# Last convolution of a four-layer kernel: the f16 high part written once by ScalarE, its second copy made by GpSimd

## The chip, the cores and the metric

The kernel runs on one core of a Trainium2 chip. The metric is the device time of the program in microseconds. The core has TensorE (PE, with its weight loads as PEld), VectorE (DVE), ScalarE (ACT), GpSimd (POOL) and SyncE (SP); the last here only issues transfers.

## The reference, cut to what matters

Four residual layers act on x of 8 x 16 x 512 x 512 (images, channels, rows, columns). The stage that is changed computes the third and the fourth:

```
# --- layer 2: quantized 3x3 convolution of the normalized x ---
x = x + _L2_conv_ref(_gn(x), weight_int8, scale_weight, bias)
# --- layer 3: multiplication in the frequency domain, by a 3x3 kernel, circularly padded ---
w_pad = _circular_pad(weight, H, W, k, p)
Lw = jnp.fft.fft2(w_pad * dL)
Kx = jnp.fft.ifft2(x, norm='ortho')
z = jnp.einsum('oihw,bihw->bohw', Lw, Kx)
x = x + jnp.real(jnp.fft.fft2(z, norm='ortho'))      # x inside is _gn(x)
```

The fourth layer is thus a 3x3 convolution with circular borders over the normalized x. The kernel computes it as one.

## The kernel before, in words

The first two thirds of the time (to about 4487 us) are the first two layers and statistics; the change doesn't touch them. The last stage handles the third layer (called conv2 in the code) and the fourth (conv3) for all eight images. An image is J = 64 tiles of 128 partitions (8 rows of 16 channels) by 512 columns, and X in SBUF holds one image.

A hand-written order of turns staggers the work. In turn t of image b, ScalarE, VectorE, TensorE and SyncE each do what belongs to several tiles: conv3 of image b runs over t, and conv2 of image b + 1 runs DELAY = 12 turns behind. So the first 12 turns of an image have conv3 alone, the last 12 conv2 alone, and image 7 has conv3 alone throughout. Between two images the statistics of the next are finished (var, rstd, norm3_ready). There is nothing but these functions and their semaphores; each engine runs its own in order.

Turn t on each engine, for conv3:

- ScalarE: `high` (L1551) writes the f16 high part of xn, item t - 1, into planes 0 and 2 of ring buffer `xs3` (8 slots); `normal` (L1543) writes xn of item t (f32, two buffers), after `low` of item t - 2. For conv2: `scale2` (L1529) before `high`, `load` (L1558, in every other turn, two tiles of the next image, into the X that conv3 has finished with) and `square3` (L1535) after `normal`.
- GpSimd: `circular` (L1509, L1510) copies the two border columns of xn, each as a product with a column of ones. `high` waits for it (pads3_ready).
- VectorE: `finish` (L1669, result tile, waits for conv3 and for the stored result buffer), `update` (L1656, conv2's result), `clip` (L1646), `low` (L1662: xn minus the high part, plane 1 of xs3), `quant` (L1651).
- SyncE: in odd turns `halos3`: waits for low and high of item t - 1, then transfers rows of neighbouring tiles from xs3, all three planes, into `xhalo` (L1462, L1470; L1459 at an image's first tile, L1464 to L1468 with the wrapped tile); in even turns `halos2` for conv2 (L1447, L1448); in every turn then `store` (L1476) of a finished result tile.
- TensorE: `conv2` (L1600, L1601: 4 matmuls) and `conv3` (L1613: 9 matmuls of xs3, with its planes 0 and 1; L1615: 3 of xhalo) of tile t - 6. It takes a halo half from three turns before.

So plane 2 is read by the halo transfers alone. `high` may be at most 7 tiles ahead of conv3 (conv3_done), xn has two buffers, the result four, conv3's PSUM two banks.

## Time and profile before

| | before |
|---|---|
| median of three runs | 6585.06 us (6578.19 to 6588.43) |
| profiled execution | 6585.46 us, of which the span is 6583.6 |
| busy, share of the span | PE 87%, DVE 75%, ACT 69%, POOL 41% |
| the changed line, L1551 | 520 times, 1049 ns in the mean |
| high part of the first image, last image | from 4596.9 us, to 6560.5 us |

The profile page gives the busy time of each engine, of the span in 40 slices, the transfer queues, a chain of waits followed back from the end, and groups of instructions by line. The span counts from the first to the last instruction. A matmul's recorded duration is longer than its share of the pipeline, so durations of matmuls are added only over a stretch. The chain of the page follows GpSimd through this stage as "issue" and L1509, since the inference goes by semaphores; it says little here, and the timeline is the better view.

### The profile page before, as it was taken

The numbers are of one execution on the slowest core, as the hardware profiler recorded it, in microseconds if no ns is written. First come the engines' busy times: TensorE is split into PE (matmuls) and PEld (weight loads), VectorE is DVE, ScalarE is ACT, GpSimd is POOL, SyncE is SP. The second block draws the span as 40 slices with busy tenths as digits, with TensorE's granted clock in tenths as the row PEclk, the third lists the DMA queues.
The fourth block names the chain that finished last, engine by engine and source line by source line (L and its number), as shares of the span: only waits on it lengthen the run. The fifth ranks groups of instructions, "written<-read, shape, count | busy, mean of one in ns | idle before, by whom it ended". The sixth has DMA issues, their size and how long they took to land. (4 is left out here: it accounts for less than half of the span.)

```text
span 6583.6 us, 201217 instructions
## 1 busy us (share of the span) xinstructions
PE 5696.3 (87%) x64138; PEld 3661.9 (56%) x64138; DVE 4922.5 (75%) x9721; ACT 4531.8 (69%) x8793; POOL 2724.0 (41%) x4633
## 2 busy tenths in 40 slices
PE   0389979979979989989988988994989889889889
PEld 0058748748848757756766766771433334334334
DVE  5778877877887887887887887887767667667664
ACT  2577767767767766766766547556878778778776
POOL 2165556556556555556546546550111111111111
PEclk9899989989999999999999999997999999999999
DMA  6426616615625634643642541552767667667665
GB/s 182 169 59 185 186 41 187 185 54 177 185 75 157 185 99 133 184 124 105 185 145 67 142 130 48 143 141 43 196 168 198 167 167 203 163 170 202 169 172 137
DMA packets 535623, 959.19 MB, mean 146 GB/s; under 512 B 121946, under 2 KB 126682, under 8 KB 532826
## 3 DMA queue, kind: packets, MB, share of 16 engines
q1 hardware_dynamic: 467546, 799.21, 43.9%
q10 hardware_dynamic: 67456, 151.01, 7.1%
q8 instruction: 474, 7.77, 0.5%
q14 instruction: 147, 1.20, 0.1%
HBM read 560.66 MB, written 287.60 MB: 129 GB/s over the span
## 5 line engine op out<-in xcount | busy, mean ns | idle before, releaser
L1613 PE MATMUL pC<-xs,taps 128*128 128x512 f16 x4608 | 1094.3, 382 | 105.9 <-DMA xhalo<-xs 101.4
L966 PE MATMUL pM<-gw,xh 64*128 64x256 f16 (+1 forms) x24960 | 1128.7, 244 | 0.0
L966 PEld LDWEIGHTS pM<-gw,xh 64*128 64x128 f16 x24960 | 966.8, 95 | 129.7 <-issue 3.3
L728 POOL TENSOR_TENSOR X<-X,zo 128x256 f32 (+1 forms) x512 | 371.5, 726 | 1244.1 <-DVE X L1077 1244.1
L1613 PEld LDWEIGHTS pC<-xs,taps 128*128 128x128 f16 x4608 | 448.8, 98 | 668.8 <-DVE xs L1662 88.3
L1509 POOL TENSOR_TENSOR xn<-xn,one_col 128x1 f32<-128x1 f32 x520 | 159.4, 307 | 1401.0 <-ACT xn L1543 1401.0
L1529 ACT ACTIVATE scaled<-X,qbias,qscale 128x512 f32 (+1 forms) x512 | 411.0, 804 | 344.9 <-DMA X<-after_layer 284.7
L272 PE MATMUL pM<-X,mix0s 64*64 64x512 f32 x2304 | 528.4, 633 | 133.9 <-DVE X L1049 108.3
L1077 DVE SCALAR_TENSOR_TENSOR X<-pZ,X 128x512 f32 (+1 forms) x512 | 353.8, 691 | 327.3 <-ACT zo L787 326.1
L1551 ACT ACTIVATE xs<-xn 128x1028 f16<-128x1028 f32 x520 | 545.7, 1049 | 73.5 <-POOL xn L1510 72.2
L713 POOL TENSOR_TENSOR X<-X,rl 128x512 f32 x384 | 478.2, 1275 | 269.4 <-ACT rl L758 269.0
L787 ACT ACTIVATE zo<-pZ 128x256 f32<-128x256 f32 x512 | 196.7, 384 | 551.1 <-PE pZ L918 551.1
L1669 DVE SCALAR_TENSOR_TENSOR result<-pC,X 128x512 f32<-128x512 f32 x512 | 352.1, 688 | 297.5 <-DMA out_dram<-result 205.7
L1600 PE MATMUL pC<-q,taps 128*128 128x512 f16 x1536 | 436.5, 394 | 126.4 <-DMA qhalo<-q 98.5
L1091 DVE TENSOR_TENSOR xt<-pT,xt 128x512 f16<-128x512 f32 x520 | 357.0, 686 | 250.5 <-ACT xt L817 248.5
L1662 DVE TENSOR_TENSOR xs<-xn,xs 128x514 f16<-128x514 f32 x520 | 359.5, 691 | 228.1 <-ACT xs L1551 224.1
L817 ACT ACTIVATE xt<-pT 128x512 f16<-128x512 f32 x520 | 310.6, 597 | 283.8 <-PE pT L930 280.2
L272 PE MATMUL pP<-X,sumw 64*64 64x512 f32 x2048 | 465.7, 593 | 0.0
L758 ACT ACTIVATE rl<-pM,relu_b,relu_s 128x512 f32<-128x512 f32 x384 | 285.4, 776 | 248.1 <-DVE X L1043 234.7
L918 PE MATMUL pM<-fwd_odd,xt 128*128 128x256 f16 x3120 | 436.2, 277 | 5.6 <-DVE xh L1102 5.6
L1543 ACT ACTIVATE xn<-X,bs,rs 128x512 f32 (+1 forms) x520 | 416.7, 801 | 32.7 <-DVEq L1708 24.2
L838 ACT ACTIVATE yt<-pM 128x512 f16<-128x512 f32 x520 | 311.1, 598 | 174.1 <-PE pM L974 173.2
(241 smaller groups left out, 13755.0 us busy)
## 6 DMA issues: line engine op xcount, KB each, us to landing
gw<-row_weights SPq DMA_DIRECT2D x520, 288.0 KB, 3.1
after_layer<-X SPq DMA_DIRECT2D x512, 256.0 KB
out_dram<-result SPq DMA_DIRECT2D x512, 256.0 KB
X<-in_x_dram SPq DMA_DIRECT2D x448, 256.0 KB
X<-after_layer ACTq DMA_DIRECT2D x224, 512.0 KB, 5.8
stage<-in_x_dram SPq DMA_DIRECT2D x192, 512.0 KB
xhalo<-xs SPq DMA_DIRECT2D x504, 96.4 KB, 3.7
qhalo<-q SPq DMA_DIRECT2D x496, 96.2 KB, 4.0
```

The costliest lines, as they stand in the source:

```text
L272: return nc.tensor.matmul(dst[c * HP:(c + 1) * HP], left, Xf[r * HP:(r + 1) * HP, j], start=start, stop=stop)
L713: nc.gpsimd.tensor_tensor(Xf[:, j], Xf[:, j], rl[:, k], ALU.add).then_inc(added_pool, 1)
L728: nc.gpsimd.tensor_tensor(X[:, j, 0], X[:, j, 0], zo[:, k], ALU.add)
L918: m = nc.tensor.matmul(dst, left(p), right(q), start=first and n == 0, stop=last and n == 2)
L966: nc.tensor.matmul(pY[:, r, col:col + nd * P], row(xh, r)[:, k, p, ri, off:off + P], weights(r, q_, d, nd, ri), start=ri == 0 and off == 1 ...
L1091: nc.vector.tensor_tensor(xt[:, k, 1], pT[:, :], xt[:, k, 0], ALU.subtract).then_inc(xt_lo, 1)
L1529: nc.scalar.activation(scaled[:, k % 4], Xf[:, w], ACT.Identity, bias=qbias[:, bass.ds(b, 1)], scale=qscale[:, bass.ds(b, 1)]).then_inc(sc ...
L1543: nc.scalar.activation(xn[:, k % 2, 1:W + 1], Xf[:, tile], ACT.Identity, bias=bs3[:, :], scale=rs3[:, :]).then_inc(xn_ready, 1)
L1551: nc.scalar.activation(xs[:, 0:3:2, k], xn[:, (k - 1) % 2].unsqueeze(1).broadcast_to([P, 2, W + 2]), ACT.Copy).then_inc(hi_ready, 1)
L1600: nc.tensor.matmul(pC2[:, slot % 4], taps2[:, d], q[:, k, d:d + W], start=d == 0, stop=False)
L1613: nc.tensor.matmul(bank, taps3[:, d, wh], xs[:, h, own, d:d + W], start=d == 0 and n == 0, stop=False)
L1662: nc.vector.tensor_tensor(xs[:, 1, k], xn[:, (k - 1) % 2], xs[:, 0, k], ALU.subtract).then_inc(lo_ready, 1)
```

## The change

`high` writes plane 0 alone (514 elements a partition instead of 1028). A new function `again` on GpSimd waits for it and writes plane 2 as plane 0 times a column of ones, broadcast over 514 columns; it stands ahead of `circular` of the next item. `halos3` waits for `again` where it waited for `high`. The wait for `low` stays. The whole diff:

```
@@ -1398,6 +1398,7 @@
                     s_("xn3_ready"), s_("pads3_ready"), s_("hi3_ready"), s_("lo3_ready"), s_("conv3_done"), s_("x4_ready"))
                 xhalo_in = [s_(f"xhalo_in{k}") for k in range(4)]
                 wrap_in = s_("wrap_in")
+                again_ready = s_("again3_ready")
                 out_stored = [s_(f"out_stored{k}") for k in range(4)]
                 loaded2 = [s_(f"loaded2_{k}") for k in range(2)]
                 CONV2_CREDIT = RING - 1
@@ -1454,7 +1455,7 @@
 
                         src = (k - 1) % RING
                         sp.wait_ge(lo_ready, b * ITEMS + t)
-                        sp.wait_ge(hi_ready, b * ITEMS + t)
+                        sp.wait_ge(again_ready, b * ITEMS + t)
                         if isinstance(t, int) and t == 1:
                             sp.dma_start(xhalo[0:3 * C, 1], xs[P - C:P, :, 1]).then_inc(xhalo_in[0], 16)
                             return
@@ -1510,13 +1511,20 @@
                         nc.gpsimd.tensor_tensor(xn[:, k, W + 1:W + 2], xn[:, k, 1:2], one_col[:, :],
                                                 ALU.mult).then_inc(pads3_ready, 1)
 
+                    def again(b, i, slot):
+                        pool.wait_ge(hi_ready, b * ITEMS + i + 1)
+                        nc.gpsimd.tensor_tensor(xs[:, 2, slot], xs[:, 0, slot], one_col[:, :].broadcast_to([P, W + 2]),
+                                                ALU.mult).then_inc(again_ready, 1)
+
                     with pool.Fori(0, B) as b:
                         pool.wait_ge(var_ready, b + 1)
                         nc.gpsimd.tensor_tensor(rstd[:, :], var[:, 1:2], half_pow[:, :], ALU.pow).then_inc(rstd_done, 1)
                         circular(b, 0, 0)
                         with pool.Fori(0, J // RING) as g:
                             for k in range(RING):
+                                again(b, g * RING + k, (k + 1) % RING)
                                 circular(b, g * RING + k + 1, (k + 1) % 2)
+                        again(b, J, 1)
 
                 @block.scalar
                 def _(act):
@@ -1548,7 +1556,7 @@
                         if not (isinstance(i, int) and i < RING):
 
                             act.wait_ge(conv3_done, b * J + i - (RING - 1))
-                        nc.scalar.activation(xs[:, 0:3:2, k], xn[:, (k - 1) % 2].unsqueeze(1).broadcast_to([P, 2, W + 2]), ACT.Copy).then_inc(hi_ready, 1)
+                        nc.scalar.activation(xs[:, 0, k], xn[:, (k - 1) % 2], ACT.Copy).then_inc(hi_ready, 1)
 
                     def load(b, w, k, g):
 
```

## Rows read from the trace of the kernel before

**Rows 1.** Windows of an image and the last: us, busy and count by engine, PEclk, DMA.
```profile
5928.00:5966.00 38.00, 35.15 (x160) 15.30 (x160) 27.00 (x59) 29.22 (x45) 4.81 (x20) 1.00 0.76 197
5966.00:6110.00 144.00, 142.40 (x655) 63.19 (x656) 109.21 (x247) 126.52 (x206) 22.39 (x78) 1.00 0.75 207
6445.00:6575.00 130.00, 130.00 (x602) 58.26 (x601) 62.17 (x96) 85.02 (x91) 14.92 (x90) 1.00 0.59 141
```

**Rows 2.** Waits of ScalarE (total, times, longest); timeline (start, us) of loads and scaled.
```profile
ACT scaled L1529 <- DMA X<-after_layer: 284.7, 167, 5.3
...
5913.97 0.81 ACT L1529 ACTIVATE scaled<-X,qbias,qscale 128x512 f32<-128x512 f32 x1 [0.78 <-DMA X<-after_layer]
5914.55 0.40 ACTq L1558 DMA_DIRECT2D X<-after_layer  x1
...
5920.58 0.81 ACT L1529 ACTIVATE scaled<-X,qbias,qscale 128x512 f32<-128x512 f32 x1 [1.61 <-DMA X<-after_layer]
```

**Rows 3.** Timeline of an image's start, conv3 alone.
```profile
5893.52 1.06 ACT L1551 ACTIVATE xs<-xn 128x1028 f16<-128x1028 f32 x1 [0.44 <-POOL xn L1510]
...
5895.36 0.19 POOL L1509 TENSOR_TENSOR xn<-xn,one_col 128x1 f32<-128x1 f32 x1 [1.88 <-ACT xn L1543]
...
5895.73 1.06 ACT L1551 ACTIVATE xs<-xn 128x1028 f16<-128x1028 f32 x1 [0.44 <-POOL xn L1510]
...
5898.27 3.94 PE L1613 MATMUL pC<-xs,taps 128*128 128x512 f16 x9 [12.64 <-DMA xhalo<-xs]
```

**Rows 4.** Groups by line and form (busy us, mean ns); L336: min/median/max ns.
```profile
L1551 ACT ACTIVATE xs<-xn 128x1028 f16<-128x1028 f32 x520 | 545.7, 1049 | 73.5 <-POOL xn L1510 72.2 <-PE pC L1615 0.5
...
L787 ACT ACTIVATE zo<-pZ 128x256 f32<-128x256 f32 x512 | 196.7, 384 | 551.1 <-PE pZ L918 551.1
...
L1543 ACT ACTIVATE xn<-X,bs,rs 128x512 f32<-128x512 f32 x200 | 160.1, 800 | 24.7 <-DVEq L1708 24.2 <-DVE xs L1662 0.5
...
L336 POOL TENSOR_TENSOR gbuf<-comph,maskh x64: 1145/1147/1323, 11.7 to 223.3; 128x576 f16<-128x576 f16 x64
...
L713 POOL TENSOR_TENSOR X<-X,rl 128x512 f32 x384 | 478.2, 1275 | 269.4 <-ACT rl L758 269.0
```

**Rows 5.** GpSimd beside VectorE: timeline at 439 us, one group, timeline at 4655 us.
```profile
439.11 0.69 DVE L1067 TENSOR_TENSOR zo<-zo,rhi 128x512 f32<-128x512 f32 x1
439.49 0.90 POOL L717 TENSOR_TENSOR even<-rl 128x256 f32<-128x256 f32 x1 [3.26 <-ACT rl L773]
439.83 0.83 DVE L1068 TENSOR_SCALAR zo<-zo,lo_slot 128x512 f32<-128x512 f32 x1
...
L728 POOL TENSOR_TENSOR X<-X,zo 128x256 f32 x448 | 325.0, 726 | 1051.7 <-DVE X L1077 1051.7
...
4655.32 0.69 DVE L1662 TENSOR_TENSOR xs<-xn,xs 128x514 f16<-128x514 f32 x1
4655.41 0.65 POOL L1510 TENSOR_TENSOR xn<-xn,one_col 128x1 f32<-128x1 f32 x1
```

**Rows 6.** Timeline of the last image.
```profile
6401.00 1.06 ACT L1551 ACTIVATE xs<-xn 128x1028 f16<-128x1028 f32 x1 [0.44 <-POOL xn L1510]
...
6560.48 1.06 ACT L1551 ACTIVATE xs<-xn 128x1028 f16<-128x1028 f32 x1 [0.44 <-POOL xn L1510]
...
6564.21 0.64 SPq L1462 DMA_DIRECT2D xhalo<-xs  x1
...
6570.48 2.11 PE L1613 MATMUL pC<-xs,taps 128*128 128x512 f16 x9
```

**Rows 7.** Transfers, 4600 to 6390 us: count, KB, median us to landing.
```profile
xhalo<-xs SPq DMA_DIRECT2D x441, 96.4 KB, 3.8
```

**Rows 8.** VectorE, a turn in the middle of an image: clip, finish, clip.
```profile
5980.26 0.42 DVE L1646 TENSOR_SCALAR scaled<-scaled 128x512 f32<-128x512 f32 x1
...
5981.87 0.69 DVE L1669 SCALAR_TENSOR_TENSOR result<-pC,X 128x512 f32<-128x512 f32 x1 [0.25 <-DMA out_dram<-result]
...
5983.14 0.42 DVE L1646 TENSOR_SCALAR scaled<-scaled 128x512 f32<-128x512 f32 x1
```

More of the change, by code:

```diff
@@ L1400, in program @@
                 wrap_in = s_("wrap_in")
+                again_ready = s_("again3_ready")
                 out_stored = [s_(f"out_stored{k}") for k in range(4)]
@@ L1456, in halos3 @@
                         sp.wait_ge(lo_ready, b * ITEMS + t)
-                        sp.wait_ge(hi_ready, b * ITEMS + t)
+                        sp.wait_ge(again_ready, b * ITEMS + t)
                         if isinstance(t, int) and t == 1:
@@ L1511, in circular, with again @@
                                                 ALU.mult).then_inc(pads3_ready, 1)
+                    def again(b, i, slot):
+                        pool.wait_ge(hi_ready, b * ITEMS + i + 1)
+                        nc.gpsimd.tensor_tensor(xs[:, 2, slot], xs[:, 0, slot], one_col[:, :].broadcast_to([P, W + 2]),
+                                                ALU.mult).then_inc(again_ready, 1)
                     with pool.Fori(0, B) as b:
@@ L1518, in _ @@
                             for k in range(RING):
+                                again(b, g * RING + k, (k + 1) % RING)
                                 circular(b, g * RING + k + 1, (k + 1) % 2)
+                        again(b, J, 1)
                 @block.scalar
@@ L1550, in high @@
                             act.wait_ge(conv3_done, b * J + i - (RING - 1))
-                        nc.scalar.activation(xs[:, 0:3:2, k], xn[:, (k - 1) % 2].unsqueeze(1).broadcast_to([P, 2, W + 2]), ACT.Copy).then_inc(hi_ready, 1)
+                        nc.scalar.activation(xs[:, 0, k], xn[:, (k - 1) % 2], ACT.Copy).then_inc(hi_ready, 1)
                     def load(b, w, k, g):
```

## The prediction

> **What bounds the kernel now.** I read the busy shares by slice first: only the last quarter (from 4490 us) has the change in it, and there TensorE is busy, GpSimd idle. Then the windows of one image, which show the same thing in numbers: in the middle of the image TensorE is busy for 142.4 of 144 us, ScalarE 126.5, VectorE 109.2, GpSimd 22.4 [rows 1]. A turn (one tile of the last convolution and one of the next image's third layer) is 16 matmuls, so it costs 142.4 / 655 x 16 = 3.48 us of TensorE; that is the floor of the middle, and it is nearly reached. The earlier stretch has 2.85 us of idle TensorE in 38 [rows 1]. The two windows hold 182 us with 4.45 of idle TensorE; over the some 220 us between an image's first matmul and its tail, that makes 5.4.
>
> What else is tight was read from the waits of ScalarE: its longest is for the load of X, 284.7 us over the seven images that load [rows 2]. The timeline shows the ring: scaled at 5913.97, the next load issued at 5914.55, the next scaled released by that load at 5920.58 after 1.61 us of idling, and so on [rows 2]. Scaled, the high part (L1551), xn (L1543) and the squares follow one another on ScalarE; where it waits for a load, a shorter L1551 buys nothing.
>
> At the start of an image there is no third-layer work for 12 turns. The timeline shows another ring there: high part at 5893.52, then xn on ScalarE, the two border columns on GpSimd from 5895.36, the next high part at 5895.73 [rows 3]: 2.21 us a turn, and TensorE's first matmuls come at 5898.27, after 12.64 us of idling for the halo [rows 3]. In the last image too there is no other layer: 12 matmuls a turn, 130.0 / 602 x 12 = 2.59 us [rows 1].
>
> **What is removed.** 520 times L1551 goes from 1028 to 514 elements. It costs 1.049 us; a Copy of 256 costs 0.384 [rows 4], so (1.049 - 0.384) / 772 = 0.86 ns an element and 0.61 us for 514. The other end is L1543, 512 elements in 0.80 us [rows 4]; I take 0.61, from the row of the same line. That is 0.44 us a turn off ScalarE, in total 229 us of busy time, nearly all beside other work: ScalarE has 126.5 / 144 of the middle and waits for loads.
>
> **What is added.** 520 products of 128x514 on GpSimd, f16 by a broadcast column of f32. No such instruction is in the trace. Below: the f16 product of 576 elements, 1.147 us, scaled to 1.02. Above: the f32 sum of 512, 1.275 [rows 4], 1.28. The new one has one operand of each kind; I take the middle, 1.15. A gain is excluded: the instruction is new, and GpSimd does nothing shorter for it.
>
> The Trainium skill (GPSIMD Engine Reference, Instruction dispatch) gives about 2.5 cycles an element at 1.2 GHz as the floor of two-input operations, by which 514 elements would be an estimated 1.07 us of loop alone and the whole about 1.28. The f16 row lies under that floor (1.147 for 576), so the trace disagrees for f16; by the page the sum below would end at its upper bound.
>
> **How it shares with VectorE.** The timeline around 439 us is the row that matters most: L717 on GpSimd is issued at 439.49 while VectorE's L1067, with two SBUF inputs, runs to 439.80, and ends at 440.39, 0.59 us after it; and L1068 on VectorE, issued at 439.83, ends 0.27 us after L717 has [rows 5]. They take turns whole, and the one that waits goes next. An instruction of its size alone takes 0.73 (L728), so 0.14 us of a GpSimd instruction is hidden while it queues. In the stage itself a one-column product issued at 4655.41, normally 0.19 us, took 0.65, up to just after the end of low (L1662, 4655.32 to 4656.01), and before quant [rows 5].
>
> The new copy and low are released by the same high part. So: high 0.61, gap 0.03 (as between 439.80 and 439.83 [rows 5]), low 0.69, copy 1.15 - 0.14 = 1.01, border columns and gap, 5895.36 to 5895.73, 0.37 [rows 3]: the ring is **2.71 us** instead of 2.21. It holds whichever of low and copy goes first. With 1.02 and 1.28 for the copy it is 2.58 and 2.84.
>
> **Start of each image.** From the first high part to turn 12 are 11 rings: 11 x 0.50 = 5.5 us. From this comes the 0.78 us that scaled then waited for its load anyway [rows 2]: the load ring starts 4.7 us later. TensorE needs less: it goes at 2.59 a turn, so it would have overtaken the old ring only by little, and its halos came in time. Ends: nothing, if TensorE's lead hides it all, and 4.7. I take 3.5, nearer to the upper end since the load ring, too, runs at about TensorE's pace and gives nothing back; seven images: **24.5 us**.
>
> **Last image.** First high part at 6401.00, the last (64 rings later) at 6560.48 [rows 6]. By the new ring: 6401.0 + 64 x 2.71 = 6574.4. Low and copy bring the halo transfer's issue to 6574.4 + 0.61 + 0.03 + 0.69 + 1.01 = 6576.8 (before: 6564.21), landing 3.8 later by the median [rows 7], 6580.6. Tile 62, which needs it, began at 6570.48 [rows 6]: **10 us** later. With 2.58: 2 us; with 2.84: 18.
>
> **The new wait.** SyncE waited for low and high; now for low and copy, 1.01 us later where low goes first. Queued behind it on SyncE are the two halo transfers (three at an image's end, with the wrap one) and then the store of a result tile. Halos are wanted three turns later, 10.4 us, against 3.8 landing, so the middle hides it. The store is tighter: L1669 already waited 0.25 us for an out_dram transfer at 5981.87 [rows 8]. But VectorE has slack in every turn (below). On GpSimd the border columns are queued behind the copy, and the next high part behind these; in the middle, again 2.71 plus one quant (about 0.3), 3.0 < 3.48: hidden, at 0 us. If TensorE's cover went, this ring would be the floor. On VectorE, quant stands behind the copy by about 1 us; qhalo follows from it, wanted three turns later as well.
>
> **Sum.** 24.5 + 10 = 34.5. The profiled execution took 6585.46 us (span 6583.6, 1.9 around it), the median is 6585.06; they stand 0.4 apart, so the sum is laid on the median: 6585 + 35 = **6620 us**, 0.5% slower. Its own range: with a copy of 1.02 (ring + 0.37) and half of the lag hidden, 7 x 0.5 x (11 x 0.37 - 0.78) + 2 = 13; with 1.28 (ring + 0.63) and none hidden, 7 x (11 x 0.63 - 0.78) + 18 = 61: 6598 to 6646.
>
> **Rivals.** *Absorbed:* TensorE's queue of finished tiles hides the slower ring at each start and nearly all of it in the last image; then only some us are left and the time is 6585, within 13. For it: TensorE is the bound [rows 1]; against: in the last image the new ring is over TensorE's turn by itself.
>
> *Faster:* ScalarE catches up sooner after each late load, so the 5.4 us of TensorE pauses in an image shrink to 1.4: 7 x 4 = 28 us less, and the start ring costs little since the copy turns out short: 6557. Against it: the pauses go with the load (L1529's wait), not with L1551.
>
> *Slower, through VectorE:* every copy holds back clip, low or quant for its whole 1.01 us. A turn of VectorE back to back is 5980.26 to 5983.14 less 0.25 of waiting, 2.63 [rows 8]; with the copy 3.64, over TensorE's 3.48. The point from which it decides is 0.85 us of holding a turn. Some 53 turns of seven images at 0.16: 59 us, and the 35 above: 6679. For it: the whole-instruction turns of [rows 5]; against it: finish and update, 5981.87 to 5983.14 [rows 8], 1.27 us of a turn, have one operand in PSUM by the code, unlike L1067 and L1068, and a late VectorE moves the copy into them. The Trainium skill (SBUF — State Buffer, Who interferes with whom) says the same of the pair: an exclusive lock, the second to issue fully blocks, also for a VectorE instruction with two SBUF inputs against a GpSimd one that reads. By that rule, the trace agrees, and by its letter alone this rival's time would hold.
>
> *Not what it says:* the broadcast operand makes the copy far dearer, 2 us say; then the ring is 3.6 us, over every floor, and the time beyond 6700.
>
> **How the numbers follow.** Forecast 0.45, absorbed 0.20, faster 0.13, through VectorE 0.18, dear copy 0.04. About 0.2% (13 us) is what a measurement of this kernel can tell from no change. Faster by more 0.13; within 0.19 (the absorbed case, little of the forecast's lower end); slower 0.68. The range leaves out the dear copy and half of the faster case and holds the rest: 6565 to 6690; it takes in the VectorE case with 11 us to spare.
>
> **What would show it.** Starts of high parts in the first ten turns 2.71 us apart instead of 2.21 (right), 2.2 (absorbed). The copy's mean between 1.02 and 1.28. GpSimd's copy beginning with or just after low and ending about 1.0 after low's end. In the last image pairs of high parts 5.4 apart and TensorE idle for the halo; in the middle TensorE still at 3.48 a turn. Low or quant well over their 0.69 and 0.42 while TensorE idles would show the VectorE case. The forecast is wrong if GpSimd reads a broadcast or mixed operands at another rate, or if the slower start costs TensorE more than the delay itself: its first nine matmuls after the pause took 3.94 us [rows 3], twice the 9/12 x 2.59 = 1.94 of later ones [rows 1], and more pauses could prolong that.

## The result, and the profile after

The changed kernel takes 6639.8 us against 6582.6 us of the kernel before in the same session: ratio 1.0083, 95% interval 1.0068 to 1.0098. It is 57 us slower by the medians and 55 by the ratio; 6620 was forecast, from 6565 to 6690. The profiled execution of after took 6637.14 us, with a span of 6634.9.

The page of the kernel after: span, busy time by engine, and the groups of the copy (L1516), the high part (L1559), low (L1670) and finish (L1677); behind the bar stand the busy time, the mean in ns, and the idle time before with what ended it.

```profile
span 6634.9 us, 201809 instructions
...
L1516 POOL TENSOR_TENSOR xs<-xs,one_col 128x514 f16<-128x514 f16 x520 | 649.6, 1249 | 728.9 <-ACT xs L1559 728.9
...
L1559 ACT ACTIVATE xs<-xn 128x514 f16<-128x514 f32 x520 | 325.1, 625 | 208.6 <-POOL xn L1511 198.9
...
L1670 DVE TENSOR_TENSOR xs<-xn,xs 128x514 f16<-128x514 f32 x520 | 398.5, 766 | 164.8 <-ACT xs L1559 138.1
...
L1677 DVE SCALAR_TENSOR_TENSOR result<-pC,X 128x512 f32<-128x512 f32 x512 | 350.6, 685 | 246.1 <-DMA out_dram<-result 231.9
```

The high part went from 1049 ns to 625 as forecast (0.61), and ScalarE now idles before it for the border columns of GpSimd 198.9 us, where it was 72.2 [rows 4]. The same windows of an image and of the last one as in [rows 1], 31 and 47 us later, since the image itself is later (us, then busy time and count of PE, PEld, DVE, ACT, POOL, then clock, DMA share, GB/s):

```profile
5959.00:5997.00 38.00, 36.02 (x166) 15.71 (x165) 33.77 (x57) 25.48 (x45) 21.29 (x33) 1.00 0.76 198
5997.00:6141.00 144.00, 135.99 (x622) 59.23 (x621) 124.02 (x235) 107.04 (x196) 75.92 (x118) 1.00 0.74 195
6492.00:6622.00 130.00, 130.00 (x600) 57.32 (x599) 75.46 (x98) 63.32 (x95) 86.67 (x142) 1.00 0.59 137
```

ScalarE has become 19 us lighter in the 144, GpSimd 54 heavier, and VectorE 15 us heavier though it has not one instruction more. TensorE is busy for 136.0 of 144 instead of 142.4: the middle of the image, which the forecast had left untouched, loses time. The last image stays full.

So that each stretch can be compared, I cut every kernel's trace at the same four events: the first high part of an image, the first matmul of the last convolution on tile 11 and that on tile 64, and the next image's first high part. "Start" is the first stretch summed over the seven images that have a neighbour, "middle" the second, "tail" the third, "last" runs from the last image's first high part to the end of its last `finish`. TensorE's floor of the middle is 53 turns x 7 x 3.48 = 1291 us. "Ring" is the distance of high parts in an image's first ten turns. All of it is one profiled execution each, the last two columns are from the timed runs.

| kernel | ring | start | middle | tail | last | median us | ratio, 95% |
|---|---|---|---|---|---|---|---|
| before | 2.23 | 281.9 | 1324 | 198 | 178.2 | 6582.6 | 1 |
| after | 2.61 | 307.8 | 1345 | 198 | 182.3 | 6639.8 | 1.0083 (1.0068 to 1.0098) |
| e1 border columns first | 2.1 | 282.5 | 1323 | 198 | 178.7 | 6585.3 | 1.0003 (0.9989 to 1.0017) |
| e2 copy aside | 2.61 | 306.7 | 1339 | 204 | 182.8 | 6641.7 | 1.0088 (1.0065 to 1.0112) |
| e3 copy of 2 | 1.9 | 262.5 | 1329 | 200 | 177.7 | 6569.0 | 0.9975 (0.9961 to 0.9989) |
| e11 no copy | 1.9 | 265.1 | 1337 | 199 | 177.5 | 6565.8 | 0.9976 (0.9966 to 0.9986) |
| e12 copy twice | 3.61 | 389.0 | 1458 | 204 | 249.3 | 6896.8 | 1.0482 (1.0462 to 1.0503) |
| e4 quant first | 2.61 | 303.0 | 1310 | 195 | 183.0 | 6581.3 | 0.9984 (0.9970 to 0.9998) |
| e5 before, quant first | 2.24 | 288.8 | 1308 | 198 | 178.0 | 6567.2 | 0.9971 (0.9957 to 0.9985) |
| e8 border and quant first | 2.1 | 284.4 | 1317 | 198 | 178.6 | 6574.6 | 0.9985 (0.9974 to 0.9995) |
| e6 split transfers | 1.9 | 269.6 | 1292 | 196 | 179.0 | 6538.7 | 0.9940 (0.9922 to 0.9958) |
| e7 split, quant first | 1.9 | 266.0 | 1319 | 200 | 177.1 | 6570.4 | 0.9980 (0.9971 to 0.9989) |
| e9 before, extra ahead of quant | 2.23 | 291.2 | 1395 | 211 | 178.4 | 6701.3 | 1.0177 (1.0162 to 1.0193) |
| e10 before, extra behind quant | 2.23 | 290.1 | 1354 | 208 | 178.2 | 6654.9 | 1.0105 (1.0088 to 1.0122) |

Each ratio is against the kernel before on the same chip, so two kernels of the table are best compared by their ratios; 0.001 is 6.6 us. From before to after the start takes 25.9 us more, the last image 4.1 and the middle 21; with the tails (0.4 less) and the stretch ahead of the first high part (0.7 more) that is the 51.3 us between the two profiled spans. A single execution is a rough gauge of the middle: the profiled one of e11 stands 15 us over its own median, that of e4 11. So I also use the timed runs: what is left of a median's difference once start and last image are taken off it. For after that is 57.2 - 25.9 - 4.1 = 27.2 us by the medians. The middle therefore costs 21 to 27, where 27 is a remainder and no measurement of its own.

**The start.** The timeline of after (start, us, engine, line; in brackets the idle time before and what ended it):

```profile
5919.61 0.63 ACT L1559 ACTIVATE xs<-xn 128x514 f16<-128x514 f32 x1 [0.44 <-POOL xn L1511]
...
5922.18 0.63 ACT L1559 ACTIVATE xs<-xn 128x514 f16<-128x514 f32 x1 [1.24 <-POOL xn L1511]
...
5924.76 0.63 ACT L1559 ACTIVATE xs<-xn 128x514 f16<-128x514 f32 x1 [1.24 <-POOL xn L1511]
...
5925.42 0.69 DVE L1670 TENSOR_TENSOR xs<-xn,xs 128x514 f16<-128x514 f32 x1 [1.88 <-ACT xs L1559]
5925.47 1.55 POOL L1516 TENSOR_TENSOR xs<-xs,one_col 128x514 f16<-128x514 f16 x1 [0.74 <-ACT xs L1559]
5926.98 0.18 POOL L1510 TENSOR_TENSOR xn<-xn,one_col 128x1 f32<-128x1 f32 x1
5927.12 0.18 POOL L1511 TENSOR_TENSOR xn<-xn,one_col 128x1 f32<-128x1 f32 x1
5927.34 0.63 ACT L1559 ACTIVATE xs<-xn 128x514 f16<-128x514 f32 x1 [1.24 <-POOL xn L1511]
...
5930.04 4.02 PE L1621 MATMUL pC<-xs,taps 128*128 128x512 f16 x9 [13.43 <-DMA xhalo<-xs]
```

In these turns it is the forecast's ring: high part, low and copy together, border columns, next high part, 2.58 us a turn instead of 2.21 [rows 3]. Low and the copy are released by the same event and begin within 0.05 us; the copy ends at 5927.02, 0.91 us after low. Then come L1510 and L1511, and 0.04 us after these the high part. TensorE's first matmuls come after 13.43 us of idling instead of 12.64. Of the rest, a good part reaches TensorE through VectorE: conv3 must wait until `finish` has emptied its bank, and `finish` is queued behind low. Within the seven starts TensorE's pauses for `finish` grow from 4.4 to 14.2 us, those for the two halos from 72.4 to 85.3.

**The last image.** Timeline of after:

```profile
6448.11 0.63 ACT L1559 ACTIVATE xs<-xn 128x514 f16<-128x514 f32 x1 [0.44 <-POOL xn L1511]
...
6478.00 2.11 PE L1621 MATMUL pC<-xs,taps 128*128 128x512 f16 x9 [1.28 <-DVE result L1677]
...
6614.93 0.63 ACT L1559 ACTIVATE xs<-xn 128x514 f16<-128x514 f32 x1 [1.19 <-POOL xn L1511]
...
6617.26 0.64 SPq L1463 DMA_DIRECT2D xhalo<-xs  x1
...
6621.51 2.11 PE L1621 MATMUL pC<-xs,taps 128*128 128x512 f16 x9
```

64 rings take 166.8 us instead of 159.5 [rows 6]: 2.61 a turn, beside TensorE's 2.59. The image gets 4.1 us longer (the 4.7 in the expectation of e1 was counted to two different events). Of these, 3.4 us are there by tile 11, in three pauses of TensorE: 1.3 us more before its first matmul, 0.8 for the next halo, 1.3 for `finish` at 6478.00. Up to tile 41 nothing is added. In the kernel before, the high part itself has fallen back to TensorE's 2.6 a turn by turn 30, so the ring of 2.61 takes hardly anything from the rest of the image.

**The middle.** Timeline of after, VectorE and GpSimd beside each other:

```profile
6000.10 0.42 DVE L1654 TENSOR_SCALAR scaled<-scaled 128x512 f32<-128x512 f32 x1
...
6000.50 0.69 DVE L1670 TENSOR_TENSOR xs<-xn,xs 128x514 f16<-128x514 f32 x1
6000.54 1.55 POOL L1516 TENSOR_TENSOR xs<-xs,one_col 128x514 f16<-128x514 f16 x1 [3.08 <-ACT xs L1559]
...
6001.11 1.27 DVE L1659 TENSOR_SCALAR q<-scaled 128x512 f16<-128x512 f32 x1
...
6002.40 0.59 SPq L1448 DMA_DIRECT2D qhalo<-q  x1
...
6003.39 1.04 POOL L1516 TENSOR_TENSOR xs<-xs,one_col 128x514 f16<-128x514 f16 x1 [0.83 <-ACT xs L1559]
6003.56 1.15 DVE L1654 TENSOR_SCALAR scaled<-scaled 128x512 f32<-128x512 f32 x1
...
6007.53 0.82 PE L1608 MATMUL pC<-q,taps 128*128 128x512 f16 x3 [1.03 <-DMA qhalo<-q]
```

The copy waits for low, goes next, and holds quant (1.27 us instead of 0.42). One turn later it begins first and holds clip (1.15 instead of 0.42). Issuing qhalo's transfer follows from quant, and TensorE waits for it, 5.15 us after the end of that quant. By form over the whole stage, and what TensorE waited for there (us, times, longest); in the kernel before that wait was 72.4 us in 57 times:

```profile
L1654 DVE TENSOR_SCALAR scaled<-scaled 128x512 f32<-128x512 f32 x448 | 290.3, 648 | 78.0 <-ACT scaled L1537 77.6
L1659 DVE TENSOR_SCALAR q<-scaled 128x512 f16<-128x512 f32 x448 | 265.0, 591 | 2.4
```

```profile
PE pC L1608 <- DMA qhalo<-q: 87.0, 77, 4.2
```

VectorE was held for 205 us in all in the stage (clip 101, quant 77, low 27; the sum of what each instruction lasted over its undisturbed 0.42 or 0.69). That is 205 / 448 = 0.46 us a turn. It came in 304 pieces of 0.67 us on average.

Within the middle alone TensorE idles 28.2 us in before and 42.6 in after. Of the 14.4 more, 8.9 are pauses for qhalo, 4.1 pauses for `update` (conv2's result not yet read by VectorE) and 1.1 for xhalo. The remaining 6.4 of the 21 us lie in the recorded durations of the same 5936 matmuls.

### The profile page after: what moved, and what is told of

Same layout as the page of the kernel before. It is cut to its first block and busy times, and to the rows that moved or that the text cites. A ratio compares the mean times of both kernels' runs of the same rounds, so it can differ in the third digit from the quotient of the medians.

```text
span 6634.9 us, 201809 instructions
## 1 busy us (share of the span) xinstructions
PE 5702.8 (86%) x64138; PEld 3656.2 (55%) x64138; DVE 5125.0 (77%) x9721; ACT 4324.3 (65%) x8793; POOL 3453.5 (52%) x5153
## 5 line engine op out<-in xcount | busy, mean ns | idle before, releaser
L1516 POOL TENSOR_TENSOR xs<-xs,one_col 128x514 f16<-128x514 f16 x520 | 649.6, 1249 | 728.9 <-ACT xs L1559 728.9
L1677 DVE SCALAR_TENSOR_TENSOR result<-pC,X 128x512 f32<-128x512 f32 x512 | 350.6, 685 | 246.1 <-DMA out_dram<-result 231.9
L1670 DVE TENSOR_TENSOR xs<-xn,xs 128x514 f16<-128x514 f32 x520 | 398.5, 766 | 164.8 <-ACT xs L1559 138.1
L1559 ACT ACTIVATE xs<-xn 128x514 f16<-128x514 f32 x520 | 325.1, 625 | 208.6 <-POOL xn L1511 198.9
L717 POOL TENSOR_TENSOR even<-rl 128x256 f32<-128x256 f32 x520 | 380.6, 732 | 106.2 <-ACT rl L773 74.4
```

The costliest lines, as they stand in the source:

```text
L717: nc.gpsimd.tensor_tensor(even[:, k], xn[:, k, 0:HALF], xn[:, k, HALF:W], ALU.add).then_inc(even_done, 1)
L1516: nc.gpsimd.tensor_tensor(xs[:, 2, slot], xs[:, 0, slot], one_col[:, :].broadcast_to([P, W + 2]), ALU.mult).then_inc(again_ready, 1)
L1670: nc.vector.tensor_tensor(xs[:, 1, k], xn[:, (k - 1) % 2], xs[:, 0, k], ALU.subtract).then_inc(lo_ready, 1)
```

## Experiments: where the ring comes from

**e1, the border columns ahead of the copy.** The same instructions as after; two of GpSimd's change places.

```diff
                             for k in range(RING):
-                                again(b, g * RING + k, (k + 1) % RING)
                                 circular(b, g * RING + k + 1, (k + 1) % 2)
+                                again(b, g * RING + k, (k + 1) % RING)
```

> Edit: on GpSimd the border columns of item i + 1 come ahead of the copy of item i, so the next high part no longer waits for the copy; all else as in the changed kernel. The changed kernel's trace has 3.2 to 3.6 us more up to each image's twelfth high part and 4.7 us more in the last image (ring 2.61 us in the place of 2.23), and, of 57 us, some 25 in the middle of the images, not yet placed. Theory ring: the start and the last image give back about 7 x 3.4 + 5 = 29 us, and the middle stays: 6611 us (6605 to 6620), ring at most 2.3 us. Rival, GpSimd's ring also slows the middle: then nearly all is given back, 6583 to 6595. Rival, the start costs nothing by itself: above 6630.

Measured: 6585.3 us, ratio 1.0003 (0.9989 to 1.0017). All 57 us are gone. The ring at the start is 2.02 to 2.20 us by the image (1.78 in the turn shown), the start 282.5 and the last image 178.7, as in the kernel before. Timeline of e1, an image's start:

```profile
4596.39 0.63 ACT L1559 ACTIVATE xs<-xn 128x514 f16<-128x514 f32 x1 [0.44 <-POOL xn L1511]
...
4597.81 0.19 POOL L1510 TENSOR_TENSOR xn<-xn,one_col 128x1 f32<-128x1 f32 x1 [0.45 <-ACT xn L1551]
...
4598.09 1.04 POOL L1516 TENSOR_TENSOR xs<-xs,one_col 128x514 f16<-128x514 f16 x1
4598.17 0.63 ACT L1559 ACTIVATE xs<-xn 128x514 f16<-128x514 f32 x1 [0.44 <-POOL xn L1511]
```

The high part now goes as soon as the border columns are there (the first ends at 4598.00), and the copy runs beside it. The middle's loss is gone too (1323 against 1324). My expectation of 6611, in which the middle kept its loss, was wrong; the value that came is the rival's, by which GpSimd's ring slows the middle as well. The second thing e1 shows speaks against the simple story of holding. Groups of e1 over the stage, by form:

```profile
L1654 DVE TENSOR_SCALAR scaled<-scaled 128x512 f32<-128x512 f32 x448 | 373.3, 833 | 45.2 <-ACT scaled L1537 45.1
L1659 DVE TENSOR_SCALAR q<-scaled 128x512 f16<-128x512 f32 x448 | 198.3, 443 | 2.4
```

Clip is held more than in after (833 ns against 648), quant hardly (443 against 591). In all VectorE is held 240 us, more than the 205 of after, and the middle costs nothing. The copy isn't free in e1, though: against e11 below, which has none, e1 is 18 us slower by the ratios (1.0003 - 0.9976), and its starts are 17 us longer (282.5 against 265.1). It gives up just what ScalarE gained.

**e2, the copy to the side, and SyncE's wait as before.** GpSimd does the same work, but nobody waits for it but GpSimd itself; the third plane holds zeros.

```diff
-                        sp.wait_ge(again_ready, b * ITEMS + t)
+                        sp.wait_ge(hi_ready, b * ITEMS + t)
...
-                        nc.gpsimd.tensor_tensor(xs[:, 2, slot], xs[:, 0, slot], one_col[:, :].broadcast_to([P, W + 2]),
+                        nc.gpsimd.tensor_tensor(aside[:, :], xs[:, 0, slot], one_col[:, :].broadcast_to([P, W + 2]),
```

> Edit: GpSimd's copy goes to a buffer of its own that nobody reads, and the halo transfer waits for the high part as before the change; plane 2 keeps zeros from the start, so the part of the halo product that uses it is left out. The copy's time, its place in the ring and its hold on the port stay; only SyncE's new wait is gone. Theory port and ring: no change against the changed kernel, 6640 us (6632 to 6646). Rival, the later halo and store transfers cost the middle its 25 us: 6610 to 6618.

Measured: 6641.7 us, 1.0088 (1.0065 to 1.0112), no different from after. The intervals of the two runs leave room for some 18 us either way, so the 25 us of the rival are excluded, and a small cost of SyncE's new wait is not. The loss is in GpSimd's time. Ring 2.61, start 306.7.

**e3, a copy of two elements.** The instruction, its waits and its place stay, its length goes.

```diff
-                        nc.gpsimd.tensor_tensor(xs[:, 2, slot], xs[:, 0, slot], one_col[:, :].broadcast_to([P, W + 2]),
+                        nc.gpsimd.tensor_tensor(xs[:, 2, slot, 0:2], xs[:, 0, slot, 0:2], one_col[:, :].broadcast_to([P, 2]),
```

> Edit: the copy takes 2 columns instead of 514; every wait and order stays, SyncE's wait for it too; the other columns of plane 2 keep zeros, so that part of the halo product is left out. Theory port and ring: the 57 us go with the copy's 0.85 us, and ScalarE's shorter high part is left: 6565 to 6583 us; ring about 0.63 + 0.69 + 0.2 + 0.4 = 1.9 us. Rival, the waits in themselves (semaphores, SyncE): above 6600.

Measured: 6569.0 us, 0.9975 (0.9961 to 0.9989), within what was expected. With the length gone, what is left is ScalarE's gain: the ring is 1.9 us and the start 262.5, 19 us under that of before. Quant and clip are undisturbed.

**e11, no copy at all.** After without L1516, the third plane again zeros.

```diff
-                        sp.wait_ge(again_ready, b * ITEMS + t)
+                        sp.wait_ge(hi_ready, b * ITEMS + t)
...
-                                again(b, g * RING + k, (k + 1) % RING)
                                 circular(b, g * RING + k + 1, (k + 1) % 2)
-                        again(b, J, 1)
```

> Edit: ScalarE writes the high part once, there is no copy, the halo transfer waits for high and low as before the change and is one transfer of three planes; plane 2 keeps zeros from the start, so that part of the halo product is left out. It parts the gain of the split transfers (6539 us) into ScalarE's shorter instruction and the split. Theory, the shorter instruction gives the start only: as the short copy, 6562 to 6575 us, and the split gave some 30 us by itself. Rival, the tiny copy and SyncE's wait had eaten the gain: 6535 to 6550.

Measured: 6565.8 us, 0.9976 (0.9966 to 0.9986), as expected and equal to e3. So ScalarE's shorter high part by itself is worth some 16 us (0.0024), and it earns them at the image starts (265.1 against 281.9). The copy therefore costs some 70 us gross (1.0083 - 0.9976), and e3 shows that it is its length that costs, not one more instruction and its waits.

**e12, the copy twice.** After with the same product a second time ahead of it, to a buffer at the side.

```diff
                         pool.wait_ge(hi_ready, b * ITEMS + i + 1)
+                        nc.gpsimd.tensor_tensor(aside[:, :], xs[:, 0, slot], one_col[:, :].broadcast_to([P, W + 2]), ALU.mult)
                         nc.gpsimd.tensor_tensor(xs[:, 2, slot], xs[:, 0, slot], one_col[:, :].broadcast_to([P, W + 2]),
```

> Edit: the changed kernel with the copy made twice (once aside), so GpSimd's part of the ring is longer by 1.04 us. Theory, the ring is high part, low, copy, border columns: 2.6 + 1.04 = 3.6 us a turn at the start and in the last image, and over TensorE's 3.48 in the middle: start 7 x 11 x 1.0 = 77 us more, last image 64 x 1.0 = 64 more, middle 53 x 7 x (3.9 - 3.65) = 90 more, above 6800 us. Rival, in the middle and in the last image the queue of finished tiles hides GpSimd: under 6730.

Measured: 6896.8 us, 1.0482 (1.0462 to 1.0503): as expected over every floor. Timeline of e12 in the last image:

```profile
6501.23 0.63 ACT L1561 ACTIVATE xs<-xn 128x514 f16<-128x514 f32 x1 [1.21 <-POOL xn L1512]
...
6501.94 1.55 POOL L1517 TENSOR_TENSOR aside<-xs,one_col 128x514 f16<-128x514 f16 x1 [0.93 <-ACT xs L1561]
6503.45 1.22 POOL L1518 TENSOR_TENSOR xs<-xs,one_col 128x514 f16<-128x514 f16 x1
...
6505.09 0.63 ACT L1561 ACTIVATE xs<-xn 128x514 f16<-128x514 f32 x1 [0.74 <-POOL xn L1512]
```

The ring grew by 3.61 - 2.61 = 1.00 us at the start; in the turn shown it is 3.86, and over the last image's 64 turns 232.8 / 64 = 3.64. The last image grew by 249.3 - 182.3 = 67.0 us, 1.05 a turn, and the start by 81.2 us, where 64 and 77 were expected. The mechanism of the ring scales as it should. The middle grew by 113 us instead of 90.

## Experiments: where the middle's loss comes from

**e4, quant ahead of low.** In after, VectorE's order in a turn is clip, low, quant; here clip, quant, low. Quant can then not be the one that waits behind low and copy.

```diff
-                            if c3 and live(t, 1, ITEMS + 1):
-                                low(b, t - 1, k)
                             if c2 and live(u, 0, J):
                                 quant(b + 1, u, k)
+                            if c3 and live(t, 1, ITEMS + 1):
+                                low(b, t - 1, k)
```

> Edit: on VectorE quant stands before low in every turn; all else as in the changed kernel, whose trace shows quant at 1.27 us instead of 0.42 where the copy took the port between low and quant. The ring at the start is untouched (no quant there). Theory, the middle is lost through the late quant (quant, then the transfer of qhalo, then TensorE's wait, 14.2 us in an image against 9.0): 6612 to 6622 us. Rival, the middle is lost through VectorE's time as a whole (about 0.85 us held a turn, whichever instruction it hits): 6635 to 6650, with low as the stretched one.

Measured: 6581.3 us, 0.9984 (0.9970 to 0.9998), under both expectations. Quant's group in e4, and TensorE's wait for qhalo there:

```profile
L1659 DVE TENSOR_SCALAR q<-scaled 128x512 f16<-128x512 f32 x448 | 197.1, 440 | 15.4
```

```profile
PE pC L1608 <- DMA qhalo<-q: 53.7, 36, 5.3
```

The start stays slow (303.0, ring 2.61) and the last image too (183.0); the middle is 1310, 14 us below that of the kernel before. So the order doesn't only give back what the copy took, it gains something of its own.

**e5, the same order in the kernel before.** The same edit, made on before.

> Edit: the kernel before, with quant ahead of low on VectorE and nothing else. The run with quant first and the copy gave back 13 + 35 us of the middle: seven images from tile 11 to tile 64 took 1310 us, against 1345 in the changed kernel and 1324 before. Theory, what it took away is the copy's hold on quant, and the order by itself does little: 6580 to 6592 us here. Rival, the order itself is worth some 14 us in the middle, so that the hold was worth 21 and the order 14: 6563 to 6576.

Measured: 6567.2 us, 0.9971 (0.9957 to 0.9985), what the rival expected. The middle is 1308, the same as in e4. The order alone is worth 19 us by the ratio; in the profiled execution the start is 7 us longer, the middle 16 shorter and the opening stretch, up to the first high part, 6 shorter. With quant first, then, the copy leaves no trace in the middle that single executions could show: 1310 with it, 1308 without.

**e8, e1 and e4 together.**

> Edit: the changed kernel with both orders turned: border columns ahead of the copy on GpSimd, quant ahead of low on VectorE. Theory, two separate costs, ring and held quant: the start and last image give back their 31 us as in the first run, and the middle is as with quant first: 6583 - 14 = 6569 us, or down to 6555 where both orders help in the middle. Rival, both edits took away the same cost (they each gave back some 57 us): then together no more than either, 6580 to 6590.

Measured: 6574.6 us, 0.9985 (0.9974 to 0.9995). The theory's 6569 lies within that interval (6566 to 6580), the rival's range at its edge, so the run doesn't decide between them. From after, though, e1 gave back 53 us and e4 65 by the ratios, and both together 65. The middle is 1317. Groups and wait of e8:

```profile
L1659 DVE TENSOR_SCALAR q<-scaled 128x512 f16<-128x512 f32 x448 | 450.3, 1005 | 15.3
```

```profile
PE pC L1608 <- DMA qhalo<-q: 54.6, 41, 4.4
```

Here the copy holds quant in 307 of 448 turns, 262 us in all, three times as much as in after (77), and TensorE waits for qhalo less than in after (54.6 against 87.0). Quant held 0.6 us a turn is not what costs.

**e9 and e10, a bystander on VectorE.** The kernel before, without any copy, with one more VectorE instruction (514 elements, 0.69 us) a turn of the third layer: in e9 just ahead of quant, in e10 just behind it. Both take the same time of VectorE; only in e9 does the quant of the same turn stand behind it.

```diff
                         dve.wait_ge(conv2_done, b * J + w + 1)
+                        extra()
                         nc.vector.tensor_scalar(q[:, (k + 5) % RING, 1:W + 1], scaled[:, k % 4], MAGIC, -MAGIC, ALU.add,
...
+                    def extra():
+                        ones_row = one_col[:, :].broadcast_to([P, W + 2])
+                        nc.vector.tensor_tensor(aside[:, :], ones_row, ones_row, ALU.subtract)
```

> Edit: the kernel before, with one more VectorE instruction of 514 elements (into a buffer of its own, from constants, some 0.6 us) between low and quant in every turn of conv2; nothing on GpSimd or ScalarE changes. So quant is late as under the copy's hold, without a copy. From tile 11 to tile 64 of seven images it took 1308 to 1310 us with quant first, 1317 with quant first and held, 1324 with low ahead, 1345 with low ahead and the copy's hold. Theory, the lateness of quant (its halo transfer is what TensorE pauses for) costs the middle: it goes to 1335 to 1350, 6595 to 6608 us in all. Rival, the middle follows something else (GpSimd, the port): 6578 to 6590.

> Edit: the same extra VectorE instruction right behind quant instead of ahead of it. VectorE has the same work, quant isn't late. Theory of the late quant: as before the change, 6578 to 6592 us, at least 10 us under the run with the instruction ahead. Rival, VectorE's time as a whole is what costs: the same time as with the instruction ahead, within 5 us.

Measured: e9 6701.3 us, 1.0177 (1.0162 to 1.0193); e10 6654.9, 1.0105 (1.0088 to 1.0122). Both are above every range given; that e10 would be at least 10 us under e9 held, by 46. TensorE's waits for qhalo over the stage, first e9, then e10:

```profile
PE pC L1601 <- DMA qhalo<-q: 140.8, 111, 4.3
```

```profile
PE pC L1601 <- DMA qhalo<-q: 111.4, 85, 5.6
```

Two parts of the miss are told apart by the cut. The opening stretch, where the third layer runs alone, got 28 and 23 us longer (first high part at 4624.5 and 4620.0 instead of 4596.9): I hadn't priced it. And the middle got 71 us longer in e9 and 30 in e10, the starts 9 and 8, the tails 13 and 10. A VectorE turn of 2.63 + 0.69 = 3.32 us is still below TensorE's 3.48, and yet costs; the same 0.69 us costs 41 us more when quant is behind it. Both have a price well before the point at which VectorE would be the bound. That the load of VectorE costs otherwise than through lateness isn't shown: in e10, too, quant ends nearer to the matmul that takes its halo than in before (table below).

## Experiments: a version without the copy

**e6, two halo transfers in place of one.** The halo needs the high part twice. The transfer can read plane 0 twice: planes 0 and 1 in one DMA (64 KB), plane 0 again in a second (32 KB), with the weight rows put in the new order. GpSimd does nothing new and ScalarE writes once; the full result is computed.

```diff
+                    def planes(dst, src, done):
+                        sp.dma_start(dst[0:2 * C], src[:, 0:2]).then_inc(done, 16)
+                        sp.dma_start(dst[2 * C:3 * C], src[:, 0]).then_inc(done, 16)
...
-                        sp.wait_ge(again_ready, b * ITEMS + t)
+                        sp.wait_ge(hi_ready, b * ITEMS + t)
...
-                            sp.dma_start(two(xhalo[0:3 * C], src, 2 * W + 4), rows(P - C, src)).then_inc(xhalo_in[src // 2], 16)
+                            planes(two(xhalo[0:3 * C], src, 2 * W + 4), rows(P - C, src), xhalo_in[src // 2])
...
-                                again(b, g * RING + k, (k + 1) % RING)
                                 circular(b, g * RING + k + 1, (k + 1) % 2)
```

> Edit: no copy at all; ScalarE writes the high part once, and each halo transfer becomes two, planes 0 and 1 to 32 partitions and plane 0 again to the other 16, with the weights' rows laid out to suit. The same output as the reference's. ScalarE's 0.42 us a turn is left without GpSimd's 1.04. Theory ring and port: start as with the short copy (19 us less than before in seven images), middle as before, 1324: 6560 to 6572 us. Rival, twice the transfers on SyncE (0.59 us each, two more in every other turn, ahead of the store) and on the queues cost more than that: above 6588.

Measured: 6538.7 us, 0.9940 (0.9922 to 0.9958): 40 us faster than before by the ratio, some 95 faster than after, and below both expectations. TensorE's waits in e6, over the stage:

```profile
PE pC L1626 <- DMA xhalo<-xs: 96.9, 23, 11.0
PE pC L1613 <- DMA qhalo<-q: 40.2, 14, 5.7
```

The middle is 1292 us, TensorE's floor of 1291. Of TensorE's pauses for qhalo within the middle 25.1 us were left in the kernel before, here 0.2. So 16 us come from ScalarE (e11), and 24 more (0.9976 - 0.9940) from the split; start and last image are no better than in e11, so these lie in the middle, though SyncE has more to issue. The traces show where qhalo's pauses go: in the middle TensorE is ready for it 6.9 us after quant in the median, against 5.2 in e11, and it lands in 4.0 us instead of 4.7 (table below). Why two smaller halo transfers bring this about stays open.

**e7, e6 with quant ahead of low.**

> Edit: as the split transfers, and quant ahead of low on VectorE. If the order is worth 14 us by itself in the middle: 6546 to 6560 us. If it only undid the copy's hold: the same as the split transfers alone, within 6 us.

Measured: 6570.4 us, 0.9980 (0.9971 to 0.9989), as neither expected, and some 26 us slower than e6 by the ratios. The pauses for qhalo stay away (0.7 us), but TensorE now pauses for xhalo, 19.4 us in 33 times, in the middle; with quant first, low and the transfer behind it are later, and the median time that xhalo has landed ahead of TensorE falls from 2.2 us to 0.9. The order that gains 19 us in the kernel before loses 26 here.

## Why the prediction was right, and where it was not

**The ring at the start: right in mechanism and nearly in size.** High part, low, copy, border columns was the chain. The copy was sized at 1.15 and measured 1.04, so the ring is 2.58 us (2.61 by the mean over the seven starts) instead of 2.71; 2.58 is what the forecast gave for a copy of 1.02. What TensorE feels of it was rated too low: the high part of turn 11 is 3.2 us later and tile 11 25.9 / 7 = 3.7 us, so none of the lag is hidden, and the 0.78 taken off for the load doesn't show. By the forecast's own sum the ring of 2.58 gives 11 x 0.37 - 0.78 = 3.3 at most. That the two errors cancel, 26 us instead of 24.5, is luck. The first nine matmuls after the pause took 4.02 us against 3.94 [rows 3], so hardly anything was added there. e1, e3 and e12 move the start with the ring and in the direction forecast.

**ScalarE's gain: taken for nothing, worth 16 us.** "Nearly all beside other work" holds in the middle, and in the ring of the start it is hidden by the copy in after. But without the copy (e3, e11) the start gains 17 to 19 us. That gain is inside the forecast's ring of 2.71, where 0.61 stands for 1.05, but its size was not told by itself.

**The last image: 4.1 us instead of 10.** The step that was off in size is the copy's length again; 2.61 instead of 2.71 over 64 turns makes the last high part 6.4 us earlier than forecast. For the cheap end of the copy 2 us was given. The place was off too: the forecast had the loss come at the end, and 3.4 of the 4.1 us are there by tile 11. The sign named for it, TensorE idle for the halo inside the last image, is missing: 130.0 of 130 busy, since at 2.61 against 2.59 its lead lasts to the end.

**SyncE's wait: 0 was forecast**, and e2 shows nothing else, within some 18 us.

**The middle: "hidden, at 0 us" was wrong; it is 21 to 27 us.** This is the term that makes 6640 out of 6620. The 57.2 us are 25.9 and 4.1 and, by subtraction, 27.2. The forecast had seen that the copy would stand between low and quant and had put quant's lateness at 1 us and at no price, three turns of cover against 3.8 us of landing. The trace shows 0.85 us of it where it happens (quant 1.27; 90 times in the stage), the clip of the next turn held as well, and qhalo's wait going from 72.4 us (57 times) to 87.0 (77).

The step that failed is the cover. Three turns are the distance in the order of turns, 10.4 us; but the traces show TensorE asking for the halo much sooner after quant than that. Timeline of before: a quant, its halo's transfer, and the matmuls that need this transfer.

```profile
5974.53 0.42 DVE L1651 TENSOR_SCALAR q<-scaled 128x512 f16<-128x512 f32 x1
...
5974.98 0.59 SPq L1447 DMA_DIRECT2D qhalo<-q  x1
...
5980.05 0.81 PE L1600 MATMUL pC<-q,taps 128*128 128x512 f16 x3
```

From quant's end to its use are 5.1 us, and the landing takes 4.1 of them. The same over the middle, from all 182 uses of a freshly landed half (medians in us, worked out from the starts, ends and landings in each trace). "Ready" is when TensorE has finished what stands before this use, counted from quant's end; "landing" counts from the transfer's issue; "ahead" is by how much the landing comes before TensorE is ready, and "late" counts the landings that come after that.

| kernel | ready | landing | ahead | late of 182 | middle |
|---|---|---|---|---|---|
| before | 4.9 | 4.2 | 0.7 | 37 | 1324 |
| after | 4.3 | 4.1 | 0.3 | 57 | 1345 |
| e1 | 4.3 | 4.0 | 0.4 | 30 | 1323 |
| e2 | 4.6 | 4.2 | 0.3 | 51 | 1339 |
| e12 | 3.7 | 4.0 | -0.3 | 112 | 1458 |
| e4 | 6.2 | 4.5 | 1.6 | 26 | 1310 |
| e5 | 6.1 | 4.6 | 1.2 | 24 | 1308 |
| e8 | 4.4 | 4.0 | 0.3 | 18 | 1317 |
| e11 | 5.2 | 4.7 | 0.6 | 52 | 1337 |
| e6 | 6.9 | 4.0 | 2.5 | 1 | 1292 |
| e9 | 3.9 | 4.1 | 0.0 | 89 | 1395 |
| e10 | 4.5 | 4.3 | 0.3 | 61 | 1354 |

So before the change 0.7 us were in hand in the median, not 6.6, and a delay of 0.85 could not be free. The middle follows the count of late landings, roughly: from 1 and 1292 us over 37 and 1324 to 112 and 1458. It doesn't follow the median alone: e8 is no further ahead than after, but few of its landings come late. The xhalo of the last convolution had 2.8 us in hand in before and 2.5 in after, so there the cover held.

**The rival through VectorE had the mechanism and not the condition.** The copy does hold VectorE, but 0.46 us a turn instead of 1.01: in 304 of 448 turns, by 0.67 us each. By its own rule (from 0.85 us on) nothing should have been lost: VectorE needn't become the bound for its lateness to reach TensorE. The Trainium skill (SBUF — State Buffer, Who interferes with whom) has the pair as an exclusive lock; the trace agrees, quant going from 0.42 to 1.27 us behind a copy of 1.04.

**What remains open.** That the middle's loss comes from the copy's length is shown (e2, e3, e11), and that it is not a fixed price of it as well (e1, e4: the same copy, no loss). That late quants cost more than an equal load of VectorE is shown without the copy (e9 against e10, 41 us). But the amount of holding doesn't predict the middle:

| kernel | VectorE held, us | of it quant | middle against before, us |
|---|---|---|---|
| after | 205 | 77 | +21 |
| e1 | 240 | 11 | -1 |
| e2 | 201 | 85 | +15 |
| e4 | 102 | 9 | -14 |
| e8 | 314 | 262 | -7 |

After and e2 fit "quant held"; e8 speaks flatly against it, with three times the holding and no loss. e1 speaks against "VectorE held". By the two orders, the middles of the single executions (and what is left of the median's difference without start and last image, by the ratio where the kernel is not after) are:

| | low ahead of quant | quant ahead of low |
|---|---|---|
| no copy | 1324 (0) | 1308 (-26) |
| border columns ahead of the copy | 1323 (+1) | 1317 (-13) |
| copy ahead of the border columns | 1345 (+27) | 1310 (-36) |

Only one of the four cells with a copy loses: the one in which both the next high part is late (behind the copy and the columns) and quant stands behind low. So it takes the two together, and either exchange heals it. The main path by which it loses is the qhalo that lands too late, by the table of landings above (8.9 of 14.4 us of additional idling in the middle); the next is `update` (4.1). Why its few tenths of a us run out in this one order, and why so few landings are late in e8, isn't resolved: how the loads of X, the two halos and the stores shift against each other was not tried by itself.

**The range.** The 6640 us lie in it, and also in the sum's own range of 6598 to 6646. But neither was made wide for a late qhalo; the one reached up for the VectorE rival, the other for a dearer copy and a start with nothing hidden. That the time fell inside with the middle at 0 is luck.

## What to carry to other kernels

When a step is moved to an idle engine, look at what is queued behind it there and who waits for that: here a 1 us copy ahead of two 0.2 us columns cost 57 us, and exchanging them gave all of it back. A cover of several turns, counted in the program's order, doesn't make lateness free in a loop that runs at 97.5% of its bound (1291 of 1324 us). Measure it in the trace, from the end of the producer to the start of the user: here it was 4.9 us and not 10.4, against 4.2 of landing, and the same 0.69 us a turn cost 30 or 71 us in the middle by where it stood, and neither was zero. And before copying data so that one transfer can read it, let two transfers read it: that version was the fastest of all, and each order of VectorE has to be tried again with it, because the order that won without it lost.

## What the runs showed of the hardware that I had not expected

- A product of 514 f16 elements by a broadcast f32 column takes 1.04 us on GpSimd when nothing is in its way, against 1.147 for 576 of pure f16 [rows 4]: 2.0 ns an element each. No cost of the broadcast operand shows. The Trainium skill (GPSIMD Engine Reference, Instruction dispatch) has 2.5 cycles at 1.2 GHz as a floor for two inputs, an estimated 1.07 us for the loop alone; the trace is below that.
- Queued behind low it lasts 1.55 us, counted from its issue, and ends 0.91 after low: some 0.13 us of it are done while it waits.
- The instruction that waits goes next, in both directions: copy after low, quant after the copy. A quant of 0.42 us lasts 1.27, and a clip of 0.42 issued when the copy is 0.17 us old lasts 1.15.
- In this kernel two halo transfers of 64 and 32 KB do better than one of 96 KB in the same place, although there are more to issue: TensorE's pauses for the other halo in the middle are 0.2 us, against 25.1 in before and 35.7 in e11, the version without a copy and with one transfer.
